# Expert blocks in the order in which tokens need them, results folded in beside the experts, layernorm statistics kept in a table

## The chip, the cores and the metric

The kernel runs on one core of a Trainium2 chip. The time is the device time of one execution in microseconds (us); less is better. TensorE (PE) multiplies matrices, VectorE (DVE), ScalarE (ACT) and GpSimd (POOL) do the rest, SyncE (SP) issues most of the DMA transfers, and POOL issues the indirect ones. The engines run their own instruction streams and meet at semaphores.

## What is computed

A macaron block on 8192 tokens of 128 features: a mixture-of-experts FFN, causal linear attention, and the same FFN again, each on a layernorm of its input and each added to the input (the FFNs by half).

```python
x = x + 0.5 * ffn(layernorm(x))
x = x + attention(layernorm(x))          # 16 heads of 8; elu+1 features; running sums over the 32 batch rows
x = x + 0.5 * ffn(layernorm(x))

def ffn(x):                              # 8 experts of width 352, the best 2 of each token; a shared expert of width 176
    top_v, top_i = top_k(x @ gate_w, 2); top_p = softmax(top_v)
    combine = zeros((T, 8)).at[arange(T)[:, None], top_i].add(top_p)
    d = einsum('tei,eih->teh', silu(x Wg) * (x Wu), Wd)
    return einsum('te,teh->th', combine, d) + (silu(x @ Sg) * (x @ Su)) @ Sd
```

## The kernel before

All tokens stay in SBUF in `X`, as 16 groups (NG) of 512 tokens; `X3(g)` is a group as four tiles (j = 0 to 3) of 128 x 128. There are five phases, with a barrier of all engines (`phase_end`, L253) between them:

- **Phase 1**, the first FFN's routing and shared expert: for each group the layernorm, the logits, the choice of two experts (`choose`), the row in its expert's region of the DRAM tensor `routed` (`place`, which adds to running counts in `base`), the scatter of rows to it by POOL (L485), and the shared expert. At its end `tables` (L1249) turns the counts into 72 entries: block n of 256 rows starts at row `row_i[n]` and belongs to expert `exp_i[n]`. Blocks stand in the order of experts.
- **Phase 2**, `experts(0)`: 71 blocks. SP loads a block (L386) up to four ahead. Of a block, PE does four transposes (L983), gate and up products (18 matmuls of 128x256) and the down products (18 of 128x128) of the block two before. ACT does the silu (L683), the high part of the hidden values (`hi`, L688), and copies the result out of PSUM (L696, L697). DVE does the copy of the transposed block (`block_in`, L1297) with the places (L1299), the low part of the hidden values (`block_low`, L1142) and the product with the silu (`block_mult`, L1292). POOL runs one small instruction (`carrier`, L494) and issues two indirect DMAs (L496) that scatter 256 rows to the DRAM tensor `result`, at the token's place.
- **Phase 3**, `streams` (L1482 on DVE, and its like on the other engines): 19 steps, m = -2 to 16. A step has the attention of group m+1 and the start of that of group m+2, and the routing and shared expert of the second FFN for groups m and m-1. Before a group comes to attention, its two expert results have to be added: SP loads them (`load_results`, L393, buffers `Y`), and group 0 and 1 are combined by DVE (`combine_first`, L1333), the others weighed by ACT (`weigh`, L656) and added by POOL (`combine`, L513). DVE then takes the mean and variance of group m+3 (`moments(1, m+3)`, L1513) and, at the head of the next step, `deviations` turns them into scale and shift.
- **Phase 4**, `experts(1)`: as phase 2, with the second routing.
- **Phase 5**: SP loads the results of a group (`load_last`), ACT weighs one half (L669), DVE multiplies the other and adds (`combine_last`, L1345), SP stores the group (L422).

The order of the work is written out by hand on each engine. In phases 2 and 4 DVE runs, for each block,

```python
block_in(n + 1, (v + 1) % XE, n + 1 - n0)
block_low(n - 1, 1 - u)
block_mult(n, u)
```

PE's next block waits for `block_in`, ACT's `hi` waits for `block_mult`, and PE's down product for `block_low`. In phase 3 POOL forms the outer products of keys and values (`outer`, L505 to L511) behind DVE's `features` (L1356), PE sums them (L945, L947), and DVE's `attend` (L1366, L1369) reads the sums.

Of the kernel before, what the change touches and what calls it, by code (L numbers as in the profile page):

```python
# [20 lines left out]
P = 128  # L21
D = 128
# [34 lines left out]
LAST = 4  # L57
XE = 4
# [3 lines left out]
def macaron(nc, x, w_attn, b_attn, w_proj, b_proj, gate_w, wg, wu, wd, sg, su, sd, out):  # L62
    ctx = ExitStack()
    with ctx:
# [62 lines left out]
        base = sb("base", [P, E])  # L127
# [6 lines left out]
        mv = sb("mv", [P, 4, NJ, 2])  # L134
        var = sb("var", [P, 4, NJ])
# [19 lines left out]
        nb = sb("nb", [P, E])  # L155
        nbi = sb("nbi", [P, E], I32)
        cum = sb("cum", [P, E])
        past = sb("past", [P, NBLK, E])
        eb = sb("eb", [P, NBLK])
        startb = sb("startb", [P, NBLK])  # L160
        rowf = sb("rowf", [P, NBLK])
        row_i = sb("row_i", [P, NBLK], I32)
# [12 lines left out]
        Y = [reused("p (j k d) -> p j k d", j=NJ, k=K, d=D) for u in range(2)]  # L175
        YL = [space[:, u * K * GT:(u + 1) * K * GT].rearrange("p (j k d) -> p j k d", j=NJ, k=K) for u in range(LAST)]
# [7 lines left out]
        num = reused("p (j h v) -> p j h v", j=NJ, h=HEADS, v=VD)  # L184
# [26 lines left out]
        PE_Y = bank(6)  # L211

# [15 lines left out]
        s_row_ends, s_padded, s_tables = sem("s_row_ends"), sem("s_padded"), sem("s_tables")  # L228

# [8 lines left out]
        s_Y = [sem("s_Y0"), sem("s_Y1")]  # L238
        s_YL = [sem(f"s_YL{u}") for u in range(LAST)]
        s_combined, s_weighed, s_deviations = sem("s_combined"), sem("s_weighed"), sem("s_deviations")  # L240
# [89 lines left out]
        def _(sp):  # L330
# [62 lines left out]
            def load_results(g, u):  # L393

                wait(sp, s_combined, g - 1)
                sp.dma_start(Y[u], results(g)).then_inc(s_Y[u], 16)

            def load_last(g, u):
                sp.dma_start(YL[u], results(g)).then_inc(s_YL[u], 16)


# [4 lines left out]
            for f in range(2):  # L406
                pads(f)
                sp.wait_ge(s_tables, f + 1)
                first_rows = [sp.value_load(row_i[0:1, m:m + 1], min_val=0, max_val=ROWS - BLK) for m in range(XE)]
                sp.drain().then_inc(s_phase, 1)  # L410
                for v in range(ROWS_AHEAD):
                    sp.wait_ge(s_scattered[v], scattered(f, v))
                fours(sp, f * NBLK, (f + 1) * NBLK, load_block(f))
                sp.drain().then_inc(s_phase, 1)
                for u in range(2):
                    sp.wait_ge(s_results[u], 16 * HALVES * (NBLK // 2 - u) * (f + 1))
                if f == 0:
                    pairs(sp, 0, NG, load_results)

            def store(g):  # L420
                sp.wait_ge(s_combined, g + (NG + 1))
                sp.dma_start(out[bass.ds(g * GT, GT), :].rearrange("(j p) d -> p j d", p=P), X3(g)).then_inc(s_stored, 16)  # L422


            for u in range(LAST):
                load_last(u, u)
            with sp.Fori(0, NG // LAST - 1) as i:
                for u in range(LAST):
                    store(i * LAST + u)
                    load_last(i * LAST + (LAST + u), u)  # L430
            for u in range(LAST):
                store(NG - LAST + u)
            sp.wait_ge(s_stored, 16 * NG)

        @block.gpsimd
        def _(pool):
# [12 lines left out]
            pool.memset(exp_i[:, NBLK:NBLK + 2], 0)  # L449
            pool.drain()  # L450
            pool.memset(pad_rows[:, :, WORDS - 2:WORDS - 1], NOTOK)
# [19 lines left out]
            pool.iota(region0[:, :], [[REGION, E]], base=0, channel_multiplier=0,  # L471
                      allow_small_or_imprecise_dtypes=True)
# [51 lines left out]
            for f in range(2):  # L524
# [3 lines left out]
                else:  # L528
                    def step(m, u, route, attend, ready, settle):
# [3 lines left out]
                        if ready:  # L533
# [3 lines left out]
                        if ready and not (isinstance(m, int) and m in (-2, NG - 3)):  # L537
                            combine(m + 3, 1 - u)
# [7 lines left out]
                    for q in range(2):  # L546
                        pool.memset(val[:, q, :, :, HD:VD], 1.0)
                    streams_of(pool, step)
# [4 lines left out]
                for u in range(2):  # L553
                    pool.wait_ge(s_results[u], 16 * HALVES * (NBLK // 2 - u) * (f + 1))
                phase_end(pool, 2 * f + 2)

        @block.scalar
        def _(act):
# [97 lines left out]
            def weigh(g, u):  # L656

                act.wait_ge(s_Y[u], (g - u) * (16 // 2) + 16)
                for k in range(K):
                    for j in range(NJ):  # L660
                        last = act.activation(Y[u][:, j, k, :], Y[u][:, j, k, :], ACT.Copy,
                                              scale=PR[:, cols(g, NJ * K, j * K + k, 1)])
                last.then_inc(s_weighed, 1)

            def weigh_last(g, u):

                act.wait_ge(s_YL[u], (g - u) * (16 // LAST) + 16)
                for j in range(NJ):
                    last = act.activation(YL[u][:, j, 1, :], YL[u][:, j, 1, :], ACT.Copy,  # L669
# [897 lines left out]
```

## Time and profile before

| what | value |
|---|---|
| median of the runs shown (3) | 1241.1 us (1237.2 to 1242.37) |
| profiled execution, from the first to the last instruction | 1240.9 us |
| PE, DVE, POOL, ACT busy | 80%, 72%, 68%, 54% |
| PE's granted clock, mean | 0.93 |
| DMA | 86.62 MB, 70 GB/s |
| phase 1, phase 2, phase 3, phase 4, phase 5 (about) | 201, 252, 498, 251, 39 us |

The profiled execution's own time is its span, 1240.9 us, and lies 0.2 us from the median, so sums made against the span stand for the median too. A row of the timeline has the start (us), the length (us), the engine, the line, the instruction, what it writes and reads, and in brackets how long the engine sat idle before it and what ended that. The start of one instruction to the start of the next is shorter than the length of the first, since an engine overlaps them; a `drain` between them takes the overlap away.

### The profile page before, as it was taken

The page shows a single profiled execution, that of the slowest core. Times are in us where ns is not written, and L with a number is a line of the kernel's source. Part 1 is how long each engine was busy: PE and PEld are TensorE (multiplying, and loading weights), DVE is VectorE, ACT ScalarE, POOL GpSimd, SP SyncE. Part 2 cuts the span into 40 slices and gives each one's busy share as a digit, 9 for nine tenths or more (in the row PEclk, how much of TensorE's full clock was granted, in tenths as well). Part 3 has the DMA queues.
Part 4 walks back from the last instruction along what each step waited for, and adds up shares of the span by engine and source line. Part 5 has one row for each costly group of instructions (what it writes and reads, how often), then busy time and mean ns, then how long its engine had stood idle before and what let it go on. Part 6 is the DMA issues. An engine that isn't in the chain of part 4 may idle for free. (4 is left out here: it accounts for less than half of the span.)

```text
span 1240.9 us, 31979 instructions
## 1 busy us (share of the span) xinstructions
PE 989.7 (80%) x8996; PEld 742.7 (60%) x8997; DVE 896.8 (72%) x2369; ACT 669.6 (54%) x1466; POOL 843.8 (68%) x872
## 2 busy tenths in 40 slices
PE   2657665999999927788888888888864999999940
PEld 1434344899989924455555555555543888899930
DVE  6778784676676745788888888888854666666748
ACT  4556642555555523466665656666331555555545
POOL 4677773777777845467787787778642677777750
PEclk9898996999999968999999999999966999999985
DMA  9411122222222221001111111100003222222229
GB/s 279 108 51 47 52 76 66 78 79 76 78 77 78 68 59 33 17 33 37 34 34 51 34 38 41 41 17 18 23 27 87 74 74 77 78 75 78 73 95 332
DMA packets 68607, 86.62 MB, mean 70 GB/s; under 512 B 13004, under 2 KB 56209, under 8 KB 68558
## 3 DMA queue, kind: packets, MB, share of 16 engines
q1 hardware_dynamic: 51278, 52.15, 14.5%
q0 software_dynamic: 17280, 33.87, 8.3%
q8 instruction: 25, 0.41, 0.1%
q14 instruction: 24, 0.20, 0.1%
HBM read 44.74 MB, written 43.04 MB: 71 GB/s over the span
## 5 line engine op out<-in xcount | busy, mean ns | idle before, releaser
L496 POOL DMA_INDIRECT expert_results<-ey,eidx x284 | 293.3, 1033 | 70.9 <-issue 69.6
L485 POOL DMA_INDIRECT routed_rows<-row,idx x256 | 255.2, 997 | 73.6 <-issue 70.2
L1142 DVE SCALAR_TENSOR_TENSOR ehT<-eh,ehT 128x768 f16<-128x768 f32 x142 | 136.1, 958 | 150.1 <-ACT ehT L688 150.1
L683 ACT ACTIVATE esil<-PSUM 128x768 f32<-128x768 f32 x142 | 115.1, 810 | 230.2 <-PE PSUM L826 224.6
L824 PE MATMUL PSUM<-eT,WGU 128*128 128x256 f16 x852 | 234.3, 275 | 1.4
L825 PE MATMUL PSUM<-eT,WGU 128*128 128x256 f16 x852 | 233.9, 275 | 0.0
L826 PE MATMUL PSUM<-eT,WGU 128*128 128x256 f16 x852 | 233.8, 274 | 0.0
L510 POOL TENSOR_TENSOR space<-qk,val 128x1152 f32<-128x1152 f32 x64 | 138.2, 2171 | 69.5 <-DVE shift L1192 48.7
L824 PE MATMUL PSUM<-WD,ehT 128*128 x852 | 161.0, 220 | 8.3 <-DVE ehT L1142 5.0
L825 PE MATMUL PSUM<-WD,ehT 128*128 x852 | 159.3, 220 | 0.0
L826 PE MATMUL PSUM<-WD,ehT 128*128 x852 | 158.8, 219 | 0.0
L945 PE MATMUL PSUM<-space,upto 128*128 128x320 f32 (+1 forms) x384 | 148.4, 496 | 9.6 <-DVE prod L1366 6.8
L1292 DVE SCALAR_TENSOR_TENSOR eh<-PSUM,esil 128x768 f32<-128x768 f32 x142 | 134.9, 950 | 8.1 <-ACT esil L683 8.1
L494 POOL TENSOR_TENSOR carrier<-ones 128x1 f32<-128x1 f32 x142 | 73.0, 514 | 72.6 <-ACT ey L697 72.6
L688 ACT ACTIVATE ehT<-eh 128x768 f16<-128x768 f32 x142 | 118.6, 835 | 2.5 <-DVE eh L1292 2.5
L945 PEld LDWEIGHTS PSUM<-space,upto 128*128 128x128 f32 x384 | 71.8, 193 | 59.7 <-issue 42.0
L1366 DVE TENSOR_TENSOR prod<-PSUM,qk 128x1152 f32<-128x1152 f32 x64 | 86.3, 1348 | 13.9 <-PE PSUM L947 9.3
L824 PEld LDWEIGHTS PSUM<-eT,WGU 128*128 x852 | 83.7, 98 | 18.8 <-issue 6.8
L824 PEld LDWEIGHTS PSUM<-WD,ehT 128*128 128x128 f16 x852 | 82.9, 97 | 14.3 <-issue 9.7
L1369 DVE TENSOR_REDUCE space<-prod 128x144 f32<-128x1152 f32 x64 | 86.6, 1353 | 5.8
L826 PEld LDWEIGHTS PSUM<-eT,WGU 128*128 x852 | 84.0, 99 | 10.4
L825 PEld LDWEIGHTS PSUM<-eT,WGU 128*128 x852 | 84.1, 99 | 7.3
(197 smaller groups left out, 2300.0 us busy)
## 6 DMA issues: line engine op xcount, KB each, us to landing
xe<-routed_rows SPq DMA_DIRECT2D x142, 130.0 KB, 2.1
space<-expert_results SPq DMA_DIRECT2D x32, 512.0 KB, 3.9
expert_results<-ey,eidx POOLq DMA_INDIRECT x284
X<-in_L_attn_x_dram SPq DMA_DIRECT2D x16, 256.0 KB, 4.6
routed_rows<-row,idx POOLq DMA_INDIRECT x256, 2.3
out_dram<-X SPq DMA_DIRECT2D x16, 256.0 KB, 4.3
routed_rows<-pad_rows SPq DMA_DIRECT2D x24, 130.0 KB
space<-in_L_ffn_Wg_dram SPq DMA_DIRECT2D x1, 1408.0 KB, 9.1
```

The source lines that it names most:

```text
L485: pool.indirect_dma_start(routed, bass.IndirectOffsetOnAxis(ap=idx[u][:, k, j:j + 1], axis=0), row[u][:, j, :], None).then_inc(s_scattered ...
L496: pool.indirect_dma_start(result, bass.IndirectOffsetOnAxis(ap=eidx[u][:, h:h + 1], axis=0), ey[u][:, h, :], None, bounds_check=K * T - 1, ...
L510: pool.tensor_tensor(kv[:, q, a, :].rearrange("p (h j i) -> p h j i", h=HEADS, j=VD), k4, v4, ALU.mult).then_inc(s_outer, 1)
L683: act.activation(esil[u][:, :], PSUM[:, 1536 * u:1536 * u + 768], ACT.Silu, scale=2.0 ** -(SX + SWT)).then_inc(s_block_silu, 1)
L688: act.activation(ehT[u][:, 0, :, :], eh32[u][:, :].rearrange("p (c t) -> p c t", c=NC), ACT.Copy).then_inc(s_block_high, 1)
L824: pe.matmul(dst, a[0], b[0], start=start, stop=False)
L825: pe.matmul(dst, a[0], b[1], start=False, stop=False)
L826: return pe.matmul(dst, a[1], b[0], start=False, stop=stop)
L945: mm = pe.matmul(PKV[:, lo:hi], upto[:, :], kv[:, q, a, lo:hi], start=True, stop=(a == 0))
L1142: return dve.scalar_tensor_tensor(out=dst, in0=src, scalar=float(2 ** scale), in1=high, op0=ALU.mult, op1=ALU.subtract)
L1292: dve.scalar_tensor_tensor(out=eh32[u][:, :], in0=PSUM[:, at:at + NC * BLK], scalar=2.0 ** (SH - SX - SWT), in1=esil[u][:, :], op0=ALU.mul ...
L1369: dve.tensor_reduce(num[:, j, :, :], prod[:, a, :].rearrange("p (h j i) -> p h j i", h=HEADS, j=VD), AX.X, ALU.add)
```

## The change

1. `place` keeps the counts after every group (`counts`, 17 sets of 8), and `tables` builds the block list in the order in which blocks are first needed: all the blocks that group 0's rows reach, then those that group 1 adds, and so on. The number of blocks is the same. The prefix sums over 128 (group, expert) pairs are done by PE, in three round trips between DVE and PE, where DVE had done them alone.
2. With that order the results of group g are complete after 4g + 11 blocks at the latest. Phases 2 and 4 load the results of groups 0 to 13 between blocks (SP, `merged`), and DVE folds groups 0 to 12 into `X` one tile a block (`combine_part`, two instructions of 128x128, while blocks 18 to 69 run). The last three groups are combined by DVE whole (`combine_rest`): after phase 2 in the first three steps of phase 3, after phase 4 in phase 5. ACT's and POOL's parts of the combinations are gone, and in phase 4 SP stores groups 0 to 11 beside the experts.
3. In phase 2 DVE also takes mean and variance of each tile that it has folded in (one `bn_stats`, one `bn_aggr` a block) and copies them to the table `kept_mv`. In phase 3 `moments(1, m+3)` becomes a copy from the table.
4. Group 0's deviations (DVE), its normalisation (ACT, `norm_high(0)`) and its low part (POOL, `low(0, ...)`) are done ahead of the barrier of phase 2, POOL's behind its wait for the last scattered rows. `num` has its own memory, no longer shared with the result buffers.

```diff
@@ sync
+            def landed(f, g):
+                if not isinstance(g, int):
+                    sp.wait_ge(s_block_results, g * NJ + (f * NBLK + COMPLETE + 3))
+                    return
+                for u in range(2):
+                    sp.wait_ge(s_results[u], 16 * HALVES * (f * (NBLK // 2 - u) + COMPLETE // 2 + 1 - u + g * (NJ // 2)))
+            def merged(f, g, u):
+                landed(f, g)
+                load_last(g, u)
+                if f and (not isinstance(g, int) or g >= 2):
+                    store(g - 2)
+            def expert_loads(f):
...
+                with sp.Fori(0, MERGED // LAST - 1) as i:
+                    for u in range(LAST):
+                        for v in range(XE):
+                            block_of(i * (LAST * XE) + (f * NBLK + 2 * LAST * XE + u * XE + v), v)
+                            if v == 2:
+                                merged(f, i * LAST + (LAST + u), u)
...
-                if f == 0:
-                    pairs(sp, 0, NG, load_results)
@@ gpsimd
-            def combine(g, u):
-                pool.wait_ge(s_weighed, g - 1)
-                for k in range(K):
-                    pool.tensor_tensor(X3(g), X3(g), Y[u][:, :, k, :], ALU.add)
-                    last = pool.drain()
-                last.then_inc(s_combined, 1)
...
+                if f == 0:
+                    low(0, xa[:, 1, :, :], 1, xa[:, 0, :, :], s_attn_high, s_attn_low)
                 phase_end(pool, 2 * f + 2)
@@ scalar
-                if ready and not (isinstance(m, int) and m in (-2, NG - 3)):
-                    weigh(m + 3, 1 - u)
...
             experts(0)
+            norm_high(0)
             phase_end(act, 2)
@@ tensor
+            def tables(f):
+                pe.wait_ge(s_fresh, f + 1)
+                pe.transpose(PT[:, 0:P], fresh[:, :], ident[:, :])
+                pe.transpose(PT[:, P:2 * P], expert_step[:, :], ident[:, :]).then_inc(s_fresh_turned, 1)
+                pe.wait_ge(s_fresh_T, f + 1)
+                pe.matmul(SUM_BEFORE, turned[:, 0:P], before[:, :], start=True, stop=True)
...
@@ vector
-                def step(n, v, ahead=True):
+                def step(n, v, ahead=True, merge=None):
                     u = v % 2
+                    first = f == 0 and merge is not None
+                    if first:
+                        combine_part(f, *merge, 0)
                     if ahead:
                         block_in(n + 1, (v + 1) % XE, n + 1 - n0)
+                    if first:
+                        dve.drain()
+                        combine_part(f, *merge, 1)
+                    elif merge is not None:
+                        combine_part(f, *merge, 0)
                     block_low(n - 1, 1 - u)
+                    if first:
+                        g, _, j = merge
+                        dve.drain()
+                        dve.bn_stats(stats[:, 1, j, :], X3(g)[:, j, :])
                     block_mult(n, u)
+                    if first:
+                        dve.drain()
+                        dve.bn_aggr(mv[:, 1, j, :], stats[:, 1, j, :])
+                        if j == NJ - 1:
+                            dve.drain()
+                            keep_moments(g)
+                    elif merge is not None:
+                        dve.drain()
+                        combine_part(f, *merge, 1)
...
+            def combine_part(f, g, u, j, k):
+                if j == 0 and k == 0:
+                    dve.wait_ge(s_YL[u], (g - u) * (16 // LAST) + (16 + f * (16 * NG // LAST)))
+                x1 = X3(g)[:, j, :]
+                last = dve.scalar_tensor_tensor(out=x1, in0=YL[u][:, j, k, :], scalar=PR[:, cols(g, NJ * K, j * K + k, 1)],
+                                                in1=x1, op0=ALU.mult, op1=ALU.add)
+                if j == NJ - 1 and k == K - 1:
+                    last.then_inc(s_combined, 1)
+            def combine_rest(f, g):
+                for k in range(K):
                     for j in range(NJ):
+                        combine_part(f, g, g % LAST, j, k)
+                    dve.drain()
...
             experts(0)
+            dve.tensor_copy(mv[:, 1, :, :], kept(0))
+            deviations(1)
             phase_end(dve, 2)
...
                 if ready:
                     features(m + 2, 0)
+                if isinstance(m, int) and m < 1:
+                    combine_rest(0, m + (MERGED + 3))
+                    moments(1, m + (MERGED + 3))
+                    dve.drain()
+                    keep_moments(m + (MERGED + 3))
+                    dve.drain()
                 if ready and not (isinstance(m, int) and m == NG - 3):
-                    dve.wait_ge(s_combined, m + 4)
-                    moments(1, m + 3)
+                    dve.tensor_copy(mv[:, 1, :, :], kept(m + 3))
...
             experts(1)
             phase_end(dve, 4)
-            with dve.Fori(0, NG // LAST) as i:
-                for u in range(LAST):
-                    combine_last(i * LAST + u, u)
+            for g in range(MERGED + 1, NG):
+                combine_rest(1, g)
```

How the instructions stand. DVE, one block in the loop of phase 2, before (`ehT` is the low part, `eh` the product with the silu, `eT` the transposed block):

```order
L1142 SCALAR_TENSOR_TENSOR ehT<-eh,ehT 128x768
L1292 SCALAR_TENSOR_TENSOR eh<-PSUM,esil 128x768
L1296 REGISTER_ALU
L1297 COPY eT<-PSUM 128x512
L1299 ISA
L1299 SCALAR_TENSOR_TENSOR places<-xe,eb 128x2
```

DVE, the same block with a tile folded in, now:

```order
L1177 SCALAR_TENSOR_TENSOR ehT<-eh,ehT 128x768
L1362 BN_STATS stats<-X 128x6
L1328 SCALAR_TENSOR_TENSOR eh<-PSUM,esil 128x768
L1366 BN_AGGR mv<-stats 128x2
L1401 ISA
L1401 SCALAR_TENSOR_TENSOR X<-space,PR,X 128x128
L1332 REGISTER_ALU
L1333 COPY eT<-PSUM 128x512
L1335 ISA
L1335 SCALAR_TENSOR_TENSOR places<-xe,eb 128x2
L1401 ISA
L1401 SCALAR_TENSOR_TENSOR X<-space,PR,X 128x128
```

Four instructions a block have come in, and three drains that these rows don't show; in phase 4 only the two at L1401 and one drain.

DVE, step m = -1 of phase 3, from its first `features` to its last `attend` of the group, before:

```order
L1359 SCALAR_TENSOR_TENSOR qk<-expo,PSUM 128x512
L1164 BN_STATS stats<-X 128x6 x4
L1167 BN_AGGR mv<-stats 128x2 x4
L1366 TENSOR_TENSOR prod<-PSUM,qk 128x1152
L1369 TENSOR_REDUCE space<-prod 128x144
```

and now:

```order
L1416 SCALAR_TENSOR_TENSOR qk<-expo,PSUM 128x512
L1401 SCALAR_TENSOR_TENSOR X<-space,PR,X 128x128 x8
L1199 BN_STATS stats<-X 128x6 x4
L1202 BN_AGGR mv<-stats 128x2 x4
L1210 COPY kept_mv<-mv 128x8
L1575 COPY mv<-kept_mv 128x8
L1423 TENSOR_TENSOR prod<-PSUM,qk 128x1152
```

In steps m = -2, -1 and 0 eight instructions and two copies stand between `features` and `attend` beside what was there; from m = 1 on only the copy at L1575 is left.

## Rows read from the trace of the kernel before

**Rows 1.** Windows, phase 2: length, busy PE, PEld, DVE, ACT, POOL, clock, DMA, GB/s

```profile
210.00:430.00 220.00, 219.28 (x2641) 197.53 (x2640) 151.02 (x265) 127.26 (x265) 166.96 (x195) 1.00 0.26 76
```

**Rows 2.** Windows of line 1292 alone (DVE, once a block), phases 2 and 4

```profile
210.00:430.00 220.00, 62.71 (x66) 1.00 0.26 76
965.00:1185.00 220.00, 62.02 (x66) 1.00 0.26 75
```

**Rows 3.** Timeline, DVE and PE, one block of phase 2

```profile
303.85 0.96 DVE L1142 SCALAR_TENSOR_TENSOR ehT<-eh,ehT 128x768 f16<-128x768 f32 x1 [0.91 <-ACT ehT L688]
304.72 0.95 DVE L1292 SCALAR_TENSOR_TENSOR eh<-PSUM,esil 128x768 f32<-128x768 f32 x1
305.59 0.41 DVE L1297 COPY eT<-PSUM 128x512 f16<-128x512 f16 x1
305.92 0.21 DVE L1299 SCALAR_TENSOR_TENSOR places<-xe,eb 128x2 f32 x1
307.14 0.96 DVE L1142 SCALAR_TENSOR_TENSOR ehT<-eh,ehT 128x768 f16<-128x768 f32 x1 [1.01 <-ACT ehT L688]
...
306.44 0.39 PE L983 MATMUL PSUM<-ident,xe 128*128 128x128 f16 x4
```

**Rows 4.** Timeline, POOL and DVE, phase 2: carrier, DMA issues, one late block

```profile
304.26 0.59 POOL L494 TENSOR_TENSOR carrier<-ones 128x1 f32<-128x1 f32 x1 [0.16 <-ACT ey L697]
305.01 1.00 POOL L496 DMA_INDIRECT expert_results<-ey,eidx  x1 [0.15 <-issue]
...
436.36 0.96 DVE L1142 SCALAR_TENSOR_TENSOR ehT<-eh,ehT 128x768 f16<-128x768 f32 x1 [1.02 <-ACT ehT L688]
436.56 1.61 POOL L496 DMA_INDIRECT expert_results<-ey,eidx  x1 [0.31 <-issue]
```

**Rows 5.** Line 1223 (DVE) in phase 3; timeline of POOL and DVE there

```profile
L1223 DVE TENSOR_TENSOR pk<-pick,posb x16: 218/631/1211, 539.4 to 934.5; 128x64 f32<-128x64 f32 x16
648.11 1.26 POOL L517 TENSOR_TENSOR X<-X,space 128x512 f32 x1
648.33 1.13 DVE L1223 TENSOR_TENSOR pk<-pick,posb 128x64 f32<-128x64 f32 x1
682.36 1.36 DVE L1366 TENSOR_TENSOR prod<-PSUM,qk 128x1152 f32<-128x1152 f32 x1 [0.18 <-PE PSUM L947]
```

**Rows 6.** Timeline, SP, DVE and PE at the head of phase 3

```profile
451.66 12.95 SPq L396 DMA_DIRECT2D space<-expert_results  x4
453.26 0.35 DVE L1532 TENSOR_SCALAR row<-row 128x4 f32<-128x4 f32 x2 [10.05 <-POOLq L255]
455.53 2.36 DVE L1339 SCALAR_TENSOR_TENSOR X<-space,PR,X 128x128 f32<-128x128 f32 x8 [1.93 <-DMA space<-expert_results]
458.01 0.87 DVE L1164 BATCH_NORM_STATS2 stats<-X 128x6 f32<-128x128 f32 x4
458.96 0.38 DVE L1167 BATCH_NORM_AGGREGATE mv<-stats 128x2 f32<-128x6 f32 x4
...
465.61 0.69 PE L831 MATMUL PSUM<-ident,xa 128*128 128x128 f16 x5 [18.69 <-POOL xa L503]
```

**Rows 7.** Timeline, SP and DVE, phase 5

```profile
1202.19 1.76 SPq L399 DMA_DIRECT2D space<-expert_results  x4
1205.94 1.14 DVE L1350 SCALAR_TENSOR_TENSOR X<-space,PR,X 128x128 f32 x4 [11.11 <-DMA space<-expert_results]
...
1237.53 0.69 DVE L1354 TENSOR_TENSOR X<-X,space 128x512 f32 x1
```

**Rows 8.** Groups by line: the weighed add of phase 5

```profile
L1350 DVE SCALAR_TENSOR_TENSOR X<-space,PR,X 128x128 f32 x64 | 18.2, 346 | 12.3 <-DMA space<-expert_results 11.8
```

**Rows 9.** Timeline, DVE and POOL, step m = -1 of phase 3

```profile
492.48 4.30 POOL L510 TENSOR_TENSOR space<-qk,val 128x1152 f32<-128x1152 f32 x2 [1.00 <-DVE qk L1359]
494.53 1.36 DVE L1366 TENSOR_TENSOR prod<-PSUM,qk 128x1152 f32<-128x1152 f32 x1 [0.89 <-PE PSUM L947]
```

**Rows 10.** Timeline, PE's first transposes of phase 2

```profile
201.26 0.58 PE L983 MATMUL PSUM<-ident,xe 128*128 128x128 f16 x4 [5.93 <-POOLq L255]
```

More of the change, by code:

```diff
@@ L412, in _ @@
                     sp.wait_ge(s_scattered[v], scattered(f, v))
[L413 to L416, printed above, removed]
-                if f == 0:
-                    pairs(sp, 0, NG, load_results)
-            def store(g):
-                sp.wait_ge(s_combined, g + (NG + 1))
-                sp.dma_start(out[bass.ds(g * GT, GT), :].rearrange("(j p) d -> p j d", p=P), X3(g)).then_inc(s_stored, 16)
-            for u in range(LAST):
[L426 to L432, printed above, removed]
+                expert_loads(f)
+            for g in range(NG - 2, NG):
+                store(g)
             sp.wait_ge(s_stored, 16 * NG)
@@ L532, in step @@
                             outer(m + 1, 1, 0)
-                        if ready:
+                        if ready and not (isinstance(m, int) and m == -2):
                             low(m + 2, xa[:, 1, :, :], 1, xa[:, 0, :, :], s_attn_high, s_attn_low)
@@ L654, in features @@
                 last.then_inc(s_qkv_parts, 1)
[L656 to L669, printed above, removed]
-                                          scale=PR[:, cols(g, NJ * K, j * K + 1, 1)])
-                last.then_inc(s_weighed, 1)
             def residual(m):
@@ L815, in _ @@
             phase_end(act, 4)
-            with act.Fori(0, NG // LAST) as i:
-                for u in range(LAST):
-                    weigh_last(i * LAST + u, u)
         @block.tensor
@@ L1072, in first_ffn @@
                     pe.wait_ge(s_weights_low, 2)
+                if edge and n == NG - 1:
+                    tables(0)
                 if not edge or n > 0:
@@ L1105, in streams @@
                         qkv_products(m + 2, 1, a)
+                if isinstance(m, int) and m == NG:
+                    tables(1)
                 if settle:
@@ L1322, in experts @@
                 block_mult(n0 + 1, 1)
-                with dve.Fori(0, (NBLK - 4) // XE) as i:
+                with dve.Fori(0, LAST) as i:
                     for b in range(XE):
                         step(i * XE + (n0 + 2 + b), (2 + b) % XE)
+                with dve.Fori(0, MERGED // LAST) as i:
+                    for g in range(LAST):
+                        for b in range(XE):
+                            step(i * (LAST * XE) + (n0 + LAST * XE + 2 + g * XE + b), (2 + b) % XE, merge=(i * LAST + g, g, b))
+                for b in range(XE):
+                    step(n0 + (LAST + MERGED) * XE + 2 + b, (2 + b) % XE, merge=(MERGED, 0, b))
                 step(n1 - 2, 2, ahead=False)
@@ L1425, in first_ffn @@
                     ends()
-                    tables()
+                    tables(0)
                 shared(n, 0)
```

158 lines of the change are left out of this document (88 added, 70 removed).

## The prediction

> **What bounds the kernel now.** I read the windows by phase first, since the phases have different limits. In the middle of phase 2, PE is busy for 219.28 of 220 us, at full clock; DVE is busy for 151.02, POOL for 166.96 [rows 1]. The line that DVE runs once a block has 66 instructions there and as many in the same stretch of phase 4 [rows 2], so both phases run at 220/66 = 3.33 us a block, and PE sets it. The timeline shows how much room DVE has. In one block its four instructions start 0.87, 0.87 and 0.33 us apart, and the last takes 0.21: 2.28 us of pitch, then 1.01 us of waiting for ACT's high part [rows 3]. So 3.33 - 2.28 = 1.05 us a block is free, but not as one piece: the copy ends at 306.00 and PE's transposes, which read it in the next round, begin at 306.44, a slack of 0.44.
>
> POOL has its own limit: `carrier` takes 0.59 us where it meets DVE's low part, and a DMA issue 1.00 [rows 4]. In the tail of the phase one issue takes 1.61 because the low part, which reads two operands from SBUF, began 0.2 us before it [rows 4]. The same happens elsewhere: 64 columns of `pk` take 218 ns at the least and 1.13 us beside POOL's two-operand add [rows 5]. A DVE and a POOL instruction that both read twice from SBUF shut each other out.
>
> At the heads of phases 3 and 5 nobody does matmuls, and the engines wait in a chain: load, combination, statistics, normalisation, transposes. PE's first transposes of phase 3 start at 465.61 after 18.69 us without work [rows 6]. Phase 5 runs from 1202.19 to the end; DVE's last add ends at 1238.22, and the span 2.7 us later [rows 7].
>
> **The change part by part**, against the profiled span of 1240.9 us.
>
> *Phase 5, -26.9.* Thirteen groups are already in `X`. What is left is a barrier and three whole groups on DVE. Phase 3's barrier shows 453.26 - 451.66 = 1.6 us from the release of SP's load to DVE's first instruction [rows 6], so DVE starts at 1202.2 + 1.6 = 1203.8. The load of the last group lands under the first two groups: it needed 3.75 us here with three others queued behind it [rows 7], and is read 5 us after DVE starts. A whole group takes DVE 2.36 us for eight instructions [rows 6], and a drain. Of that pattern I need two prices. An add of 128x128 takes 346 ns alone [rows 8] and four take 1.14 [rows 7], so a further one costs (1.14 - 0.346)/3 = 0.265. Eight with one drain inside would be 0.346 + 6 x 0.265 = 1.94 plus the step across the drain, 0.42; the drain therefore costs 0.42 - 0.265 = 0.155. Three groups: 3 x (2.36 + 0.155) = 7.5, to 1211.3, and 2.7 for the last store: 1214.0.
>
> *Head of phase 3, -11.0.* Group 0 comes normalised out of phase 2. DVE had been idle for 10.05 us there [rows 6], which covers its statistics and ACT's part. Left is POOL's low part behind the last scatter, priced by its nearest row, an operation of the same size at 1.26 [rows 5], and the barrier: 451.7 + 1.3 + 1.6 = 454.6 in place of 465.6.
>
> *Phase 2, blocks with a tile, +14.* There are 52. Each gets two adds of 128x128 (2 x 0.265), three drains (3 x 0.155), one `bn_stats` and one `bn_aggr`. Four of these take 0.87 and 0.38 [rows 6]; if the first takes what the last does in a burst, I get pitches of 0.20 and 0.08. A copy every fourth block adds 0.06. Sum 2.28 + 0.53 + 0.47 + 0.20 + 0.08 + 0.06 = 3.62, more than PE's 3.33. The order rows show nothing on DVE that could go under anything else, so DVE becomes the bound: (3.62 - 3.33) x 52 = 15, of which I keep 14.6 because the first blocks start with some lead. Ends: +6 if a drain costs no more than half of 0.155, +22 if each costs that again where ACT's work falls due late.
>
> *Phase 4, blocks with a tile, +1.5.* Two adds and one drain: 2.28 + 0.53 + 0.16 = 2.97 a block, under 3.33. But one add and one drain, 0.42, stand before the copy's successor in the loop, and the slack to the transposes is 0.44 [rows 3]. From 0 to +8 (0.15 a block).
>
> *Steps m = -2, -1, 0, +10.5.* Between `features` and `attend` DVE now has the whole combination (2.5), the statistics (1.3) and two copies with drains (0.5): 4.3 us. In step -1 POOL's two outer products take 4.30 together, 2.15 each, and DVE's wait for PE's sums behind them is 0.89 [rows 9]. So about 2.1 us can hide there: +2.2 in each of the steps -1 and 0, little in -2, 4.6 in all. The eight adds read two operands from SBUF and so do the outer products; with one of them shut out once, each step has 2 us more: 2.3 + 4.1 + 4.1 = 10.5. Ends: +4.6 with no meeting, +17 with two meetings a step.
>
> *Steps from m = 1, -2.5.* ACT's weighing, POOL's two drained adds (1.26 each [rows 5]) and DVE's 1.25 of statistics go. But `prod` already waits 0.18 us for PE's sums [rows 5]: DVE and PE hand a group back and forth, and statistics lie in that gap. What is gained is the part of `pk`'s 1.13 that was blockage, where it isn't in the gap: some 0.2 a step over 12 steps. Ends: 0, and -6 with half a microsecond each.
>
> *Nothing* for the tables. PE waits 5.93 us for POOL at the start of phase 2 [rows 10], so POOL's scatters cover DVE's and PE's sums; without that cover three round trips would show. Nothing for SP's loads between blocks: DMA has a busy share of 0.26 [rows 1], and four blocks are loaded ahead, so a load may be late by some blocks of 3.33.
>
> Sum: 1240.9 - 26.9 - 11.0 + 14.6 + 1.5 + 10.5 - 2.5 = **1227**, 14 below the median of 1241.1.
>
> **Two rules weighed.** That a drain costs 0.155 of DVE's time is worked out from rows alone. The Trainium skill, "VectorE: DVE Perf Modes", section "The DRAIN you can't avoid", says that the pipe empties after every operation anyway, so that a wait for it costs nothing extra; by that rule three drains would be free and phase 2 would stay under 3.33. The rows speak against it: the four instructions of a block start closer together than their lengths. The Trainium skill, "SBUF — State Buffer", section "Who interferes with whom", says that a vector instruction with two SBUF inputs contends with a GpSimd instruction that reads SBUF, and that a copy can take the shared pair too; the first half agrees with the 1.61 us issue and the 1.13 us `pk`, the second no row here shows.
>
> **The rivals.**
>
> A, *DVE has room.* If drains fall where DVE waits for ACT or for PE anyway, 0.47 goes and a block of phase 2 needs 3.15, under 3.33; the meetings with the outer product don't happen either. Then phases 2 and 4 add nothing and the head 4.6: 1240.9 - 37.9 - 2.5 + 4.6 = 1205, with a little lost in both, **1208**. For it: 1.01 us of waiting in each block [rows 3]. Against it: the wait ends with ACT's `hi`, which itself waits for DVE's product, so work ahead of that product delays its own release.
>
> B, *POOL becomes the bound, slower.* POOL needs per block 0.59, two issues of 1.00 and the gaps between, about 3.2. Each block gets two more instructions with two SBUF operands, 0.35 each, at places where POOL issues. If an issue is held by them as by the low part (0.6 of 1.61 [rows 4]), POOL needs about 3.2 + 0.65 = 3.85 and both phases run at that: +0.52 x 104 = 54 in place of 16, so 1227 - 16 + 54 = **1265**. It turns the sign from 3.33 + 30/104 = 3.62 us a block in both phases.
>
> C, *the copy from the table waits.* Each step now starts with a copy of 8 columns from SBUF to SBUF. If it is held for an outer product's 2.15 us, half of it shows, +1.1 in 13 steps, 14 us: **1241**. For it stands only that `pk`, as small, is held; against it that `pk` has two operands and the copy one. By the section on who interferes, a copy contends; that gives the case its chance.
>
> D, *it does not do as it says.* SP waits for the results of a group ahead of the next blocks' loads. If they come later than four blocks, PE starves once in four blocks, 1 to 3 us, 13 times: **1240 to 1260** in sum. The order guarantees 4g + 11 blocks and SP asks then, so there is room.
>
> **How the numbers follow.** Forecast 0.55, A 0.22, B 0.08, C 0.09, D 0.06. The likeliest gives 1227. Its own ends, with the terms added as independent, are 1216 and 1238. The range takes in most of A below and of C above: 1207 to 1243. A measurement of this kernel tells 0.5%, 6 us, from no change. Faster by more: the forecast but for its top end, and A, 0.74. Within: C, part of D, that top end, 0.14. Slower: B, part of C and D, 0.12.
>
> **What the profile after would show.** DVE's product, once a block, comes every 3.6 us in phase 2 while tiles are folded in and every 3.33 in phase 4; with A both show 3.33, with B both 3.8 and held issues. PE's first transposes of phase 3 start near 454.6 plus what phase 2 lost. `prod` of steps -1 and 0 waits for nothing but DVE's own queue, and adds or outer products there are as much as 2 us longer than alone. The copy from the table is under 0.2 us, or C holds. From POOL's last scatter to DVE's last add lie 9 us. Wrong in the large would be a phase 4 that grows by as much as phase 2.

## The result and the profile after

The changed kernel takes 1259.5 us (median of 4 runs, 1258.11 to 1261.77) against 1241.7 for the kernel before (1237.2 to 1242.79): a ratio of 1.0161, interval 1.0141 to 1.0181. It is slower by 18 us; the forecast was 1227, with 1207 to 1243 as the range, so the sign was wrong too.

The profiled execution spans 1256.4 us, 15.5 more than before. I cut both traces at the same events: DVE's product with the silu (once a block, 71 times a phase) and its `attend` (L1369 before, L1426 after; four a group, so a step of phase 3 is four of them).

| stretch | before | after | difference | forecast |
|---|---|---|---|---|
| start to first product of phase 2 | 207.6 | 206.8 | -0.8 | 0 |
| phase 2, first to last product | 232.8 | 260.1 | +27.3 | +14.6 |
| to the first `attend` of phase 3 | 38.6 | 28.9 | -9.7 | -11.0 + 2.3 |
| from there to the eleventh `attend` (steps m = -1 and 0 and half of 1) | 62.4 | 76.2 | +13.8 | +8.2 |
| from there to the 63rd, the steady steps | 355.3 | 358.0 | +2.8 | -2.5 |
| to the first product of phase 4 | 60.9 | 58.3 | -2.6 | 0 |
| phase 4, first to last product | 234.5 | 245.8 | +11.3 | +1.5 |
| to the end | 48.9 | 22.4 | -26.5 | -26.9 |

The windows of both phases show which engine has become short. First the changed kernel's phase 2 (length, then busy us of PE, PEld, DVE, ACT and POOL, clock, DMA share, GB/s):

```profile
280.00:430.00 150.00, 141.72 (x1551) 114.08 (x1550) 132.25 (x322) 74.52 (x156) 100.92 (x117) 1.00 0.32 102
```

Then its product alone (L1328), in phases 2 and 4:

```profile
280.00:430.00 150.00, 35.91 (x39) 1.00 0.32 102
1050.00:1190.00 140.00, 37.17 (x40) 1.00 0.41 125
```

PE was busy for 219.28 of 220 us [rows 1] and now for 141.72 of 150; DVE has risen to 132 of 150. There are 39 blocks in 150 us of phase 2 and 40 in 140 of phase 4, which is 3.85 and 3.50 us a block in place of 3.33 [rows 2]. Over just the 52 blocks with a tile, from one start to the next, it is 3.855 us in phase 2 and 3.565 in phase 4 (3.319 and 3.347 before). POOL has not become short: 101 of 150 us, less than before. The timeline of DVE for one block of phase 2 answers to [rows 3]:

```profile
347.48 0.96 DVE L1177 SCALAR_TENSOR_TENSOR ehT<-eh,ehT 128x768 f16<-128x768 f32 x1
348.53 0.29 DVE L1362 BATCH_NORM_STATS2 stats<-X 128x6 f32 x1
348.74 0.94 DVE L1328 SCALAR_TENSOR_TENSOR eh<-PSUM,esil 128x768 f32<-128x768 f32 x1
349.77 0.18 DVE L1366 BATCH_NORM_AGGREGATE mv<-stats 128x2 f32<-128x6 f32 x1
349.94 0.35 DVE L1401 SCALAR_TENSOR_TENSOR X<-space,PR,X 128x128 f32 x1
350.21 0.42 DVE L1333 COPY eT<-PSUM 128x512 f16<-128x512 f16 x1
350.54 0.21 DVE L1335 SCALAR_TENSOR_TENSOR places<-xe,eb 128x2 f32 x1
350.95 0.35 DVE L1401 SCALAR_TENSOR_TENSOR X<-space,PR,X 128x128 f32 x1 [0.19 <-issue]
351.22 0.95 DVE L1177 SCALAR_TENSOR_TENSOR ehT<-eh,ehT 128x768 f16<-128x768 f32 x1
```

The 1.01 us of waiting for ACT is gone. DVE's queue never stands still but for drains, and takes 351.22 - 347.48 = 3.74 us; a block with the copy to the table takes 4.15, so four take 15.4, 3.85 each. Phase 4, the same view:

```profile
1101.29 0.96 DVE L1177 SCALAR_TENSOR_TENSOR ehT<-eh,ehT 128x768 f16<-128x768 f32 x1 [0.54 <-ACT ehT L707]
1102.16 0.95 DVE L1328 SCALAR_TENSOR_TENSOR eh<-PSUM,esil 128x768 f32<-128x768 f32 x1
1103.31 0.35 DVE L1401 SCALAR_TENSOR_TENSOR X<-space,PR,X 128x128 f32 x1 [0.20 <-issue]
1103.85 0.42 DVE L1333 COPY eT<-PSUM 128x512 f16<-128x512 f16 x1 [0.19 <-issue]
```

Here DVE still waits for ACT, half a microsecond a block, and yet the pace has fallen. What has changed is the step from product to copy: 1103.85 - 1102.16 = 1.69 us where it was 0.87. In this block the copy was held by 0.27 more; in most blocks the step is 1.42, and its mean over phase 4 (1080 to 1200 us) is 1.44.

In step m = -1 of phase 3 (to be laid beside [rows 9] and the eight adds of [rows 6]), DVE and POOL:

```profile
509.16 0.69 DVE L1416 SCALAR_TENSOR_TENSOR qk<-expo,PSUM 128x512 f32<-128x512 f32 x1 [1.29 <-ACT val L688]
509.76 6.18 DVE L1401 SCALAR_TENSOR_TENSOR X<-space,PR,X 128x128 f32<-128x128 f32 x8
516.03 0.88 DVE L1199 BATCH_NORM_STATS2 stats<-X 128x6 f32<-128x128 f32 x4
...
517.76 1.35 DVE L1423 TENSOR_TENSOR prod<-PSUM,qk 128x1152 f32<-128x1152 f32 x1
```
```profile
509.93 4.39 POOL L553 TENSOR_TENSOR space<-qk,val 128x1152 f32<-128x1152 f32 x2 [4.65 <-DVE qk L1416]
```

Eight adds take 6.18 us in place of 2.36. Both outer products of POOL took place meanwhile, and POOL lost only 4.39 - 4.30 = 0.09 us by it. The other two combinations, in steps -2 and 0, take 6.33 and 6.18 us.

### The profile page after: what moved, and what is told of

Its sections match the earlier page's. It is cut to its first block and busy times, and to the rows that moved or that the text cites. A ratio compares the mean times of both kernels' runs of the same rounds, so it can differ in the third digit from the quotient of the medians.

```text
span 1256.4 us, 31832 instructions
## 1 busy us (share of the span) xinstructions
PE 1023.3 (81%) x9014; PEld 741.2 (59%) x9015; DVE 962.1 (77%) x2547; ACT 615.3 (49%) x1290; POOL 805.3 (64%) x847
## 5 line engine op out<-in xcount | busy, mean ns | idle before, releaser
L539 POOL DMA_INDIRECT expert_results<-ey,eidx x284 | 284.1, 1000 | 72.8 <-issue 65.6
L976 PE MATMUL PSUM<-space,upto 128*128 128x320 f32 (+1 forms) x384 | 152.9, 508 | 25.4 <-DVE prod L1423 23.6
L839 PE MATMUL PSUM<-WD,ehT 128*128 x852 | 166.6, 220 | 7.2 <-DVE ehT L1177 4.8
L840 PE MATMUL PSUM<-WD,ehT 128*128 x852 | 162.8, 220 | 0.1
L841 PE MATMUL PSUM<-WD,ehT 128*128 x852 | 162.3, 219 | 0.0
L537 POOL TENSOR_TENSOR carrier<-ones 128x1 f32<-128x1 f32 x142 | 80.1, 564 | 107.2 <-ACT ey L716 106.9
L1328 DVE SCALAR_TENSOR_TENSOR eh<-PSUM,esil 128x768 f32<-128x768 f32 x142 | 134.4, 947 | 7.4 <-ACT esil L702 7.4
L1401 DVE SCALAR_TENSOR_TENSOR X<-space,PR,X 128x128 f32 (+1 forms) x256 | 97.9, 394 | 32.4 <-issue 20.5
L839 PEld LDWEIGHTS PSUM<-eT,WGU 128*128 x852 | 83.1, 98 | 44.9 <-issue 33.5
L1426 DVE TENSOR_REDUCE num<-prod 128x144 f32<-128x1152 f32 x64 | 86.6, 1353 | 5.9
L841 PEld LDWEIGHTS PSUM<-eT,WGU 128*128 x852 | 83.7, 98 | 11.1 <-issue 0.2
```

The source lines that it names most:

```text
L537: pool.tensor_tensor(carrier[:, u:u + 1], ones32[:, 0:1], ones32[:, 0:1], ALU.mult).then_inc(s_carrier, 1)
L539: pool.indirect_dma_start(result, bass.IndirectOffsetOnAxis(ap=eidx[u][:, h:h + 1], axis=0), ey[u][:, h, :], None, bounds_check=K * T - 1, ...
L839: pe.matmul(dst, a[0], b[0], start=start, stop=False)
L840: pe.matmul(dst, a[0], b[1], start=False, stop=False)
L841: return pe.matmul(dst, a[1], b[0], start=False, stop=stop)
L976: mm = pe.matmul(PKV[:, lo:hi], upto[:, :], kv[:, q, a, lo:hi], start=True, stop=(a == 0))
```

## The experiments

Theory 1: what costs is the order of DVE's own queue; in phase 2 its sum, in phase 4 what stands ahead of the copy, in phase 3 the adds beside outer products. The rival: meetings with POOL's issues and the load of the results by DMA, which hang on the work and not on its place. Each experiment but e7, e8 and e11 is one execution beside the kernel before in the same session (1242.2 us for e1 to e4, 1242.8 for e13 and e14), so I go by the stretches of its trace as well as by its time.

**e1: statistics back in phase 3.** Phase 2 runs its blocks as phase 4 does; the table is not used.

```diff
-                    first = f == 0 and merge is not None
+                    first = False
...
-                    dve.tensor_copy(mv[:, 1, :, :], kept(m + 3))
+                    moments(1, m + 3)
```

> Phase 2 folds tiles in as phase 4 does (two adds, one drain); the statistics are taken in phase 3 from X, in every step, and the table is not used. Theory 1 (DVE's own queue is the bound of phase 2): a block with a tile goes from 3.85 us to phase 4's 3.55, 52 x 0.30 = 16 us less; the steady steps of phase 3 stay at 13.9 us a step, since the statistics lie in the gap in which DVE waits for PE's sums. Sum 1259.5 - 16 = about 1243. Rival (the price is that of the adds meeting POOL's issues, whatever else DVE does): phase 2 stays at about 3.8 and the time within 3 us of 1259. Rival on phase 3: if the table did save time there, the steady steps become 0.5 us or more longer, +6 us.

Measured: 1243.9. Phase 2 takes 244.9 us in place of 260.1, 3.552 us a block with a tile, the steady steps 357.2 in place of 358.0. The windows show PE nearer to full again:

```profile
280.00:430.00 150.00, 147.47 (x1690) 124.89 (x1688) 122.49 (x254) 81.13 (x169) 107.28 (x127) 1.00 0.37 112
```

So the statistics cost 15 us in phase 2 and gave the steady steps nothing: a step of theirs takes 27.87 and 26.97 us in turn with the statistics and without. That they lie in the time that DVE waits for PE anyway is my reading of it. (The 13.9 us a step of the expectation is half a step.) From the first to the eleventh `attend` e1 takes 79.4 us, not 76.2, but so do e3 and e14 (78.9 each), where nothing was edited there: this stretch differs by 3 us from one execution to the next.

**e2, e14, the change, e3: phase 4, with more and more ahead of the copy.** Only the place of the two adds and the drain is different. e2 has all three between places and low part:

```diff
                     elif merge is not None:
                         combine_part(f, *merge, 0)
+                        dve.drain()
+                        combine_part(f, *merge, 1)
                     block_low(n - 1, 1 - u)
...
-                    elif merge is not None:
-                        dve.drain()
-                        combine_part(f, *merge, 1)
```

e3 has all three ahead of `block_in`, e14 the first add ahead of it, the drain and the second add behind.

> Phase 4 only: both adds of a tile, with their drain, stand between the places and the low part, where DVE waits for ACT's high part; nothing is left between the product and the copy that PE's transposes wait for. Theory 1 (the place in the queue is what costs): phase 4 goes from 3.55 us a block with a tile to 3.33 to 3.37, 9 to 11 us less, to about 1249. Rival (meetings with POOL's issues, or the load of the results by DMA): the adds and the transfers are the same, so phase 4 keeps its 3.55, 1259.

> Phase 4 only: both adds and their drain stand ahead of the copy of the transposed block, so that 0.69 us comes before it instead of 0.42. Theory 1: PE's transposes are later by another 0.27 us, a block with a tile costs 3.8 us, 52 x 0.27 = 14 us more, about 1273. Rival (contention): 3.55 as now, 1259.

> Phase 4 only: one add stands ahead of the copy, with no drain there (0.27 us), the drain and the other add behind the places. With 0 ahead the blocks with a tile took 3.387 us, with 0.42 3.565, with 0.69 3.639. If the time ahead of the copy is what costs, this gives 3.45 to 3.50. Rival (a drain ahead of the copy is what costs, whatever its length): 3.39, as in e2.

| phase 4 | product to copy, mean | us a block with a tile | phase | time |
|---|---|---|---|---|
| before | 0.868 | 3.347 | 234.5 | 1241.7 |
| e2, nothing ahead | 0.867 | 3.387 | 236.1 | 1251.4 |
| e14, one add | 1.127 | 3.473 | 241.0 | 1253.9 |
| the change, drain and add | 1.441 | 3.565 | 245.8 | 1259.5 |
| e3, add, drain and add | 1.666 | 3.639 | 250.1 | 1267.6 |

Work, transfers and drains are the same in all four, so the rival falls: in phase 4 place alone is worth 14 us. e14 came as expected, e2 a little above its 3.33 to 3.37. e3's expectation was too high. Its 4.3 us in phase 4 are a third of the 14 expected; the rest of its 8 us lies ahead of phase 4, where nothing was edited (6.9 us more in its trace, of which 2.7 are between the first and the eleventh `attend`). By the table a microsecond ahead of the copy costs (3.639 - 3.387)/(1.666 - 0.867) = 0.32 us a block, and the first 0.26 costs as well. A chain over two blocks was my explanation. In e3, DVE and ACT:

```profile
1101.48 0.42 DVE L1333 COPY eT<-PSUM 128x512 f16<-128x512 f16 x1
1104.60 0.81 ACT L702 ACTIVATE esil<-PSUM 128x768 f32<-128x768 f32 x1 [1.58 <-PE PSUM L841]
1105.31 0.83 ACT L707 ACTIVATE ehT<-eh 128x768 f16<-128x768 f32 x1
1106.18 0.96 DVE L1177 SCALAR_TENSOR_TENSOR ehT<-eh,ehT 128x768 f16<-128x768 f32 x1 [0.40 <-ACT ehT L707]
1107.05 0.95 DVE L1328 SCALAR_TENSOR_TENSOR eh<-PSUM,esil 128x768 f32<-128x768 f32 x1
```

The copy at 1101.48 feeds the gate and up products, whose silu starts at 1104.60; ACT's high part, DVE's low part and product follow one another, and behind the product, 1.66 later, comes the copy after next, at about 1108.7. That is 7.2 us for two blocks, so a delay in it would count half. But it fits roughly only: without the 0.80 us ahead of the copy it would be 6.4 us, 3.2 a block and under PE's 3.33, and yet the first 0.26 costs 0.09. PE's own rows show where the time goes. In the changed kernel's phase 4, the last gate product of a block and the first up product:

```profile
1101.85 0.27 PE L841 MATMUL PSUM<-eT,WGU 128*128 128x256 f16 x1
1102.22 0.28 PE L839 MATMUL PSUM<-eT,WGU 128*128 128x256 f16 x1
```

and the same two before (phase 2):

```profile
304.28 0.27 PE L826 MATMUL PSUM<-eT,WGU 128*128 128x256 f16 x1
304.39 0.27 PE L824 MATMUL PSUM<-eT,WGU 128*128 128x256 f16 x1
```

Means over the blocks from 1080 to 1140 us, in us:

| phase 4 | last gate to first up product | last down product to transposes | first to last down product | block |
|---|---|---|---|---|
| before | 0.14 | 0.07 | 1.03 | 3.32 |
| e2, nothing ahead | 0.14 | 0.07 | 1.03 | 3.32 |
| e14, one add | 0.18 | 0.08 | 1.08 | 3.41 |
| the change | 0.28 | 0.09 | 1.10 | 3.56 |
| e3 | 0.33 | 0.12 | 1.11 | 3.64 |

So PE hardly waits for the copy: the transposes follow the down products almost as closely as before. About half or more of what a block loses is a pause between gate and up products, which grows with the time ahead of the copy, and most of the rest lies within the down products. At that pause the code has one thing more, the load of the next block's expert number into a register (`read_number`). A late copy releases PE's instructions late, and this load may then no longer be covered by matmuls issued ahead; no run takes it away, so that, and the chain, are argued. The dependence on the place is shown.

**e4: the last three groups at the border of phases 2 and 3.** Groups 13 and 14 are combined ahead of the barrier, behind group 0's deviations, and 15 behind it, each with its statistics; nothing of it is left in the steps.

```diff
             deviations(1)
+            for g in range(MERGED + 1, NG - 1):
+                rest_kept(g)
             phase_end(dve, 2)
+            rest_kept(NG - 1)
```

> The last three groups are combined, with their statistics, where DVE is idle: two ahead of the barrier of phase 2 (6.0 us idle there in the changed kernel) and one behind it (5.7 us idle ahead of the first features). Theory: adds that run beside an outer product of POOL take 6.2 us instead of 2.4 and delay the hand-off of DVE and PE; out of there the three steps lose 3.5 + 5.8 + 6.3 us, less about 2 us for what two groups (7.8 us) exceed the 6.0: about 1246. Rival (the steps -1 and 0 are slow for another cause, such as cold loads): they stay 5.8 and 6.3 us over before, and the time falls by 3 us at most.

Measured: 1244.3. From the first `attend` to the ninth, two steps, it takes 49.7 us in place of 62.4 (49.7 before), and the first `attend` comes as early behind the last product as in the change (28.8 us), though PE's transposes start 3.4 us later. The rival falls.

**e5 and e10: the same adds ahead of `features`.** They stay in their steps, but no outer product runs beside them.

```diff
+                if isinstance(m, int) and m < 1:
+                    combine_rest(0, m + (MERGED + 3))
...
                 if ready:
                     features(m + 2, 0)
```

> The combination of the last three groups stands, in the same three steps of phase 3, ahead of DVE's features instead of behind them, when POOL forms no outer product. Theory (two-operand instructions of DVE and POOL shut each other out): the eight adds take 2.4 us a group instead of 6.2, and most of the idle time ahead of features (5.7, 1.3 us) is filled: 3 x 3.8 us and some of 7 us of waiting less, against a later start of POOL's outer products; 8 to 14 us under 1259.5, about 1249. Rival (the adds are slow because of the transfers or because the rows are cold): they take 6 us here too, and the time is 1257 or more.

> The kernel of e5_rest_before_features once more, for the same reason. Theory: the eight adds take 2.4 us a group, 8 to 14 us less than 1259.5. Rival: 6 us a group, 1257 or more.

Both fell into sessions in which the kernel before itself took about 1400 us (median 1403 and 1395), with pauses of every engine, so their times (1357.7, 1356.4) say nothing of the change. The lengths of single instructions do, and the stretch from the first to the ninth `attend`, which such a session leaves as it is (49.6 us in e6, e9 and e12, 49.7 in the kernel before). DVE's timeline of e10:

```profile
554.34 2.35 DVE L1401 SCALAR_TENSOR_TENSOR X<-space,PR,X 128x128 f32<-128x128 f32 x8
579.13 2.34 DVE L1401 SCALAR_TENSOR_TENSOR X<-space,PR,X 128x128 f32<-128x128 f32 x8
```

6.2 us have become 2.35 with the same data and the same eight instructions, in e5 too, and the two steps take 51.9 us in both in place of 62.4. That the adds were shut out by POOL's outer products is shown, and that it is worth about 10 us in these steps; what e10's order makes of the whole time is not.

**e6, e9, e12, e13: drains alone.** The kernel before, with three drains a block and no other work:

```diff
                     block_in(n + 1, (v + 1) % XE, n + 1 - n0)
+                    dve.drain()
                     block_low(n - 1, 1 - u)
+                    dve.drain()
                     block_mult(n, u)
+                    dve.drain()
```

> The kernel before with three drains a block in phases 2 and 4 (behind the places, the low part and the product), and no other work. Theory 1 (a drain costs DVE 0.16 to 0.20 us where the next instruction follows closely, and nothing where DVE waits anyway): the product starts 1.05 instead of 0.87 us behind the low part, the copy 1.05 instead of 0.87 behind the product, the one behind the places is hidden; the pace goes from 3.33 to at most 3.45 us a block, +5 to +16 us over the kernel before, 1247 to 1258. Rival (a drain only names a flush that happens anyway): the starts stay 0.87 apart and the time is that of the kernel before, 1242.

> The kernel of e6_drains_alone once more, for the same reason. Theory 1: starts behind the low part and the product 1.05 instead of 0.87 us apart, pace at most 3.45, 1245 to 1258. Rival: 0.87 and 1242.

> The kernel of e6_drains_alone a third time, for its pace on a chip where the kernel before takes 1242. The starts behind the low part and the product are 1.05 and 1.12 us apart by the second run's trace, 0.43 us more in a block than before, of which DVE's wait for the high part (1.0 us) can give nothing back to the copy ahead of it: theory 1 says 3.35 to 3.45 us a block, 1245 to 1255. Rival (a drain costs nothing): 1242.

> As for e12_drains_alone_third, where the kernel before takes 1242: theory 1 3.35 to 3.45 us a block and 1245 to 1255; rival 1242.

The first three met such sessions (1398.8, 1399.1 and 1386.9, beside 1403, 1395 and 1370). The fourth gives 1268.4 beside 1242.8: 25.7 us for nothing but drains, more than I expected, at 3.533 us a block in both phases (phase 2 is 14.1 us longer, phase 4 12.4). DVE's timeline in phase 4:

```profile
1101.05 0.96 DVE L1142 SCALAR_TENSOR_TENSOR ehT<-eh,ehT 128x768 f16<-128x768 f32 x1 [0.74 <-ACT ehT L688]
1102.10 0.96 DVE L1292 SCALAR_TENSOR_TENSOR eh<-PSUM,esil 128x768 f32<-128x768 f32 x1
1103.51 0.42 DVE L1297 COPY eT<-PSUM 128x512 f16<-128x512 f16 x1 [0.45 <-issue]
```

Product to copy is 1.12 us in three blocks of four and 1.41 in the others, as here, 1.19 in the mean (0.87 before); low part to product is 1.07 in the mean (0.87 before). That is 0.32 + 0.20 = 0.52 more, and at the change's own slope in phase 4, (3.565 - 3.347)/(1.441 - 0.868) = 0.38, 0.20 us a block, as measured. PE pauses here too, 0.24 us between gate and up products. DVE still waits 0.7 us a block for ACT. Free time at one place of the queue does not pay for a drain at another.

**e7, e8, e11: all three cures.** The changed kernel with e1's statistics, e2's place for the adds in both phases, and the last three groups at the border.

> The changed kernel with both adds of a tile in the gap ahead of the low part in phases 2 and 4, the statistics in phase 3 as before the change, and the last three groups combined where DVE is idle at the border of phases 2 and 3. If the terms add: 1259.5 - 52 x (3.855 - 3.39) = -24, -9 in phase 4, -15 to -17 at the head of phase 3: 1210 (1205 to 1216), 2.5% under the kernel before. If one of the terms was only moved onto another bound (POOL's issues at 3.3 us a block), 1225 or more.

> The kernel of e7_all_three once more, since the kernel before took 1403 us there instead of 1242 and nothing can be laid beside the other runs. As for e7: if the terms add, 1210 (1205 to 1216); if POOL's issues become the bound at a little over 3.4 us a block, 1215 to 1225; if a term was only moved, 1225 or more.

> The kernel of e7_all_three a third time: twice the kernel before took about 1400 us in the same session, with pauses of every engine, so that nothing could be laid beside the other runs. As for e7, where the kernel before takes 1242: 1210 (1205 to 1216) if the terms add; 1225 or more if a term was only moved.

In the disturbed sessions of e7 and e8 it took 1337.8 and 1340.5 (ratios 0.953 and 0.958 to a kernel before of 1403 and 1395). In the third it took 1208.5 us (4 runs, 1205.56 to 1208.75) beside 1240.2: ratio 0.9737, interval 0.9714 to 0.9761, faster than both kernels. Its phase 2 takes 233.3 us and phase 4 236.4, the stretch from the first to the ninth `attend` 49.3. A block with a tile takes 3.335 and 3.392 us. The windows of phase 2 have PE back at the limit:

```profile
280.00:430.00 150.00, 149.43 (x1803) 135.01 (x1802) 130.34 (x270) 86.92 (x181) 115.78 (x135) 1.00 0.39 119
```

and DVE's timeline of a block keeps product and copy 0.87 apart, with both adds in the gap:

```profile
404.72 0.95 DVE L1328 SCALAR_TENSOR_TENSOR eh<-PSUM,esil 128x768 f32<-128x768 f32 x1
405.58 0.41 DVE L1333 COPY eT<-PSUM 128x512 f16<-128x512 f16 x1
405.92 0.21 DVE L1335 SCALAR_TENSOR_TENSOR places<-xe,eb 128x2 f32 x1
406.04 0.34 DVE L1400 SCALAR_TENSOR_TENSOR X<-space,PR,X 128x128 f32 x1
406.56 0.35 DVE L1400 SCALAR_TENSOR_TENSOR X<-space,PR,X 128x128 f32 x1 [0.17 <-issue]
407.13 0.96 DVE L1177 SCALAR_TENSOR_TENSOR ehT<-eh,ehT 128x768 f16<-128x768 f32 x1 [0.22 <-ACT ehT L707]
```

## Why the prediction was wrong

- *Phase 5 and the head of phase 3* were right: -26.5 for -26.9, and PE's transposes come 13.2 us sooner behind the last product (12.0 instead of 25.2), for -11.0.
- *Phase 2, +14.6; measured +27.3.* The mechanism was right, DVE's queue is the bound. The term that failed is the sum of that queue, too small because of its prices for drains and single instructions: 3.85 us a block for 3.62. By the timeline above, `bn_aggr` takes 0.17 up to the next start where I had 0.08. A lone one starts behind a drain and is followed by an add, and the pitch (the time from one start to the next) in a burst of four is no measure of that. The drains cost 0.18, 0.16 and 0.20 where I had 0.155 each (the 0.20 is over the length of the places instruction, 0.21; over the 0.13 us from its start to the next one's where no drain stands between, it is 0.28). The copy to the table with its drain costs 0.41 every fourth block, not 0.24. The end of +22 that I kept for this did not hold it. The three errors have one root: prices taken from bursts of like instructions were used for single ones. The ends did not follow from the prices either: three drains at half of 0.155 give 14.6 - 12 = +2.5, not +6, and three at twice that +39, which would have held the 27.3.
- *Phase 4, +1.5; measured +11.3.* The step that failed is the slack: I let 0.44 us between the copy's end and PE's transposes absorb an add and a drain. The step from product to copy grew by 0.57 (the drain behind the product of 768 columns puts the add at 1.15 instead of 0.87, and the add itself takes 0.27), and nothing absorbed it: in e14 0.26 us ahead of the copy already cost 0.09 a block. I had read the slack from one link. That link held, the transposes follow the down products after 0.09 us where it was 0.07, but PE paused behind it, by 0.14 us more between gate and up products and 0.07 within the down products. I had the link itself wrong too: the transposes do not read the copy, they overwrite the PSUM that it has read, and the gate and up products behind them read it.
- *Steps -1 and 0, with -2: +10.5; measured +17.3* (3.5 at the first `attend` beyond the transposes, 13.8 after it). Here too the mechanism was right and the size was at its other end, 17: DVE is shut out by both outer products, not by one. The Trainium skill, "SBUF — State Buffer", section "SBUF: two separate sides", says that DVE, with two inputs in SBUF, and a POOL instruction that reads SBUF share a pair of ports, and that whoever starts first has it for its whole instruction; the 6.18 us beside a POOL that lost 0.09, and e10's 2.35, agree. I took it for a chance event; in all three combinations it fell on DVE, the engine with the short instructions.
- *Steps from m = 1, -2.5; measured +2.8*, of which 2.5 are in one step. The gain was to be from blockage of `pk`; nothing came. e5 and e10 have 355.4 and 355.3 us here, as before the change, and e1 puts 1.25 us of statistics back into each step without making it longer, so this was the end of 0 that I had given.
- *The rivals.* A fell: in phase 2 DVE had no time left, in phase 4 it had, but not where it was needed. The Trainium skill, "VectorE: DVE Perf Modes", section "The DRAIN you can't avoid", says that a semaphore behind each copy costs nothing extra; the prediction read that as true of a drain, of which it does not speak. e13 has 25.7 us for drains alone. B had the sign and not the mechanism: POOL's median issue is 997 ns, 998 before. C did not come about: the copy from the table takes 160 to 172 ns in all 16 places. But in phase 3 none of its 15 runs met an instruction of POOL, so whether such a copy would be held is not shown. D: SP's waits for results starved nobody, as e11 shows with the same loads at 3.34 us a block.

I had the slower side at 0.12, and all of it on POOL and SP. The terms for phases 2 and 4, which I added as independent, had a common cause, too small a price for a drain and its surroundings, and failed together. The forecast was 14 us less than the profiled span before, and the span became 15.5 longer. Of these 29 us phase 2 is 13, phase 4 10, the first steps of phase 3 7 and the steady steps 5; the other stretches gave 5 back.

## What to carry to other kernels

Free time of an engine belongs to a place in its queue. Before you put work beside a bound engine, find which of its instructions the chain goes through, and put the work (with its drains) where the engine waits, not between an arrival and the instruction that others wait for: the same two adds a block cost phase 4 2 us or 16. Work that is moved out of a gap gains nothing there and costs in full where it lands. Keep short two-operand instructions of DVE away from POOL's long ones.

## What the runs showed of the hardware that I had not expected

- Three drains a block, with nothing else, cost 25.7 us over 142 blocks, 0.18 us a block, while DVE still waited 0.7 us in each.
- Where eight adds of DVE (0.35 us each) met two outer products of POOL (2.15 us each), DVE lost 3.8 us and POOL 0.09.
- With the copy 0.80 us later, PE's transposes still followed the down products after 0.12 us (0.07 before), but the step from gate to up products grew from 0.14 to 0.33 us.
- In some sessions the same kernel takes 1370 to 1403 us instead of 1242, and the differences between kernels change with it: the drains that cost 25.7 us otherwise cost -4, +4 and +17 there, and the kernel with all three cures gains 4 to 5% instead of 2.6%. The time is lost around and in the expert phases: the same kernel takes 47 us more up to the first product of phase 2 in e7 than in e11, 33 more in phase 2 and 51 in phase 4, and none more from the first to the last `attend` (427 and 430 us). What disturbed them I did not find out.
